# Retention and FP4 feed-forward: old state read in row halves, queries, scores and state moved up in VectorE's order

## What is computed

```python
qkv = x @ w_qkv.T                                  # q, k: 8 heads of 32; v: 8 heads of 64
q, k = xpos(q), xpos(k)                            # rotation and scale by position
ret = einsum('bhtd,bhsd->bhts', q, k) * 32**-0.5 * decay[h]**(t-s)   # for s <= t, else 0
out = einsum('bhts,bhsv->bhtv', ret, v)
y = silu(x @ w_gated.T) * (out - mean) / sqrt(var + eps) @ w_proj.T  # mean, var per head
x1 = layernorm(x + y)
# feed-forward, 704 hidden, every operand rounded to FP4 in blocks of 16 with a scale each
h = silu(q4(x1) @ q4(w_gate).T) * (q4(x1) @ q4(w_up).T)
result = layernorm(x1 + q4(h) @ q4(w_down).T)
```

## Time and profile before

| | us |
|---|---|
| median of 3 runs | 621.46 (619.71 to 621.79) |
| the profiled execution | 620.8, its span 619.0 |
| TensorE busy | 583.0 (94%), 4304 instructions |
| its weight loads | 499.7 (81%) |
| VectorE busy | 518.0 (84%), 1293 |
| ScalarE busy | 338.2 (55%), 834 |
| GpSimd busy | 226.3 (37%), 258 |
| chain that ended last | PE 48%, issue 17%, DVE 16%, ACT 12% |

### The profile page before, as it was taken

How to read it: one execution, slowest core, us unless ns; L and a number is a source line. 1 busy time by engine, 2 the same in 40 slices (tenths; PEclk the granted TensorE clock), 3 DMA queues, 4 the chain that set the end, 5 groups by cost and what they waited for, 6 DMA issues and landing times.

```text
span 619.0 us, 13802 instructions
## 1 busy us (share of the span) xinstructions
PE 583.0 (94%) x4304; PEld 499.7 (81%) x4304; DVE 518.0 (84%) x1293; ACT 338.2 (55%) x834; POOL 226.3 (37%) x258
## 2 busy tenths in 40 slices
PE   7999999999999999999999787878999999999984
PEld 3788888788878888787878666767999999999984
DVE  6668788889889888988898767888888888888896
ACT  3356566675757666676757652413444545445442
POOL 2110123343433434343433205445454455444520
PEclk9999999999999999999999978987999999999998
DMA  7610111011011101100110000000000101010002
GB/s 208 205 44 10 52 52 36 19 51 51 6 44 51 42 8 51 51 25 25 51 34 10 17 11 1 0 2 0 1 19 17 35 2 35 1 36 17 18 19 85
DMA packets 24966, 22.30 MB, mean 36 GB/s; under 512 B 2009, under 2 KB 21858, under 8 KB 24930
## 3 DMA queue, kind: packets, MB, share of 16 engines
q1 hardware_dynamic: 24114, 20.27, 10.9%
q10 hardware_dynamic: 816, 1.57, 0.8%
HBM read 17.63 MB, written 4.20 MB: 35 GB/s over the span
## 4 chain that ended last, share of the span: by engine, by line
PE 48%; issue 17%; DVE 16%; ACT 12%; POOL 3%; DMA 2%; DVEq 1%; ACTq 0%; POOLq 0%
PE wide_banks L1291 24%; PE upd_y L1291 7%; ACT shared L441 5%; PE mixed L1291 5%; PE mixed L1354 3%; PE wide_banks L1464 3%; ACT shared L456 2%; PE mixed L1347 2%; ACT squares L433 2%; DVE stats L648 1%; DVE resid L644 1%; PE wide_banks L1338 1%; POOL shared L1259 1%; POOL shared L1264 1%; ACT x_rounder L403 1%
## 5 line engine op out<-in xcount | busy, mean ns | idle before, releaser
L1264 POOL TENSOR_TENSOR shared<-shared,h_scale 128x704 f32<-128x704 bf16 x31 | 43.0, 1389 | 84.7 <-DVE shared L814 84.7
L527 ACT ACTIVATE shared<-wide_banks 128x512 f32<-128x512 f32 x64 | 29.6, 463 | 80.1 <-PE wide_banks L1291 80.1
L441 ACT ACTIVATE shared<-opened,rstd 128x64 f32<-128x64 f32 x256 | 64.7, 335 | 13.5 <-DVE rstd L727 13.1
L1291 PE MATMUL wide_banks<-wgu_hi,xq_hi 128*128 128x512 f32 (+1 forms) x192 | 61.8, 404 | 9.0 <-DVE xq_lo L1015 9.0
L1291 PE MATMUL wide_banks<-win_hi,x_hi 128*128 128x512 f32 x192 | 67.9, 435 | 0.4 <-DVE shared L637 0.4
L1354 PEld LDWEIGHTS mixed<-shared 128*128 128x128 f32 x512 | 62.0, 192 | 2.8
L1354 PE MATMUL mixed<-shared 128*128 128x64 f32 x512 | 60.6, 271 | 0.0
L1291 PE MATMUL wide_banks<-win_hi,x_lo 128*128 128x512 f32 x192 | 60.4, 396 | 0.0
L1291 PE MATMUL wide_banks<-win_lo,x_hi 128*128 128x512 f32 x192 | 60.3, 395 | 0.0
L1215 POOL TENSOR_TENSOR x_lo<-xf,x_hi 128x256 fp32r<-128x256 f32 x32 | 23.8, 743 | 99.3 <-DVE rsq L712 50.0
L1259 POOL TENSOR_TENSOR shared<-shared,h_inv 128x704 f32<-128x704 f32 x31 | 43.1, 1392 | 44.5 <-DVE h_inv L805 44.5
(11 more groups left out here) (149 smaller groups left out, 1463.6 us busy)
## 6 DMA issues: line engine op xcount, KB each, us to landing
xf<-in_x_feat SPq DMA_DIRECT2D x32, 128.0 KB, 2.2
tab<-in_tables SPq DMA_DIRECT2D x16, 256.0 KB, 2.7
xt<-in_x_tok SPq DMA_DIRECT2D x32, 128.0 KB, 2.1
out<-x SPq DMA_DIRECT2D x32, 128.0 KB, 1.7
x<-in_w_in ACTq DMA_DIRECT2D x3, 512.0 KB, 5.4
w<-in_w_gu SPq DMA_DIRECT2D x1, 1408.0 KB, 8.4
w<-in_w_down SPq DMA_DIRECT2D x1, 704.0 KB, 9.6
wgu_lo<-pow_dram SPq DMA_DIRECT2D x1, 576.0 KB, 4.5
```

The source lines that it names most:

```text
L441: last = act.activation(gated[:, b, cols], opened[:, b, cols], ACT.Copy, scale=rstd[:, b, 1 + k:2 + k])
L527: act.activation(silu[:, cols[0]:cols[1]], proj[:, part, 0:cols[1] - cols[0]], ACT.Silu).then_inc(silu_done[part], 1)
L1264: pool.tensor_tensor(over_blocks(hq[:, b]), over_blocks(h_steps[:, b]), spread(h_fp4["scale"][:, b]), ALU.mult).then_inc(h_fp4["ready"], 1)
L1291: last = pe.matmul(dst, lhs, rhs, start=k == 0, stop=k == len(parts) - 1)
```

## The change

- **State in row halves.** `state_bd` has 128 columns per group and not 256: heads 0 and 1 of a group keep rows 0 to 63, heads 2 and 3 rows 64 to 127, and both pairs use the same 128 columns. `cross` has four matmuls of 64 rows and 128 columns in place of two of 128 rows and 256 columns. The row halves r = 0 and r = 1 write different banks.
- **Banks.** `mixed` is the upper 256 columns of banks 5 and 6; `upd` is in the lower columns of bank 6; `y` is in the upper columns of bank 4, one of the scores' (for the last three tiles, in bank 6). The heads stand in another order in `mixed` (function `place`), so `gate` is read and `w_proj` is loaded (two DMAs, waited for as 32) in that order.
- **Waits.** `upd_done` is signalled by cross's last matmul and not by update's. `mix` waits for `state_summed` of the same tile; `update` waits for `opened_ready`; `scores` waits for `resid_done`, in place of `update`; `project_out` waits for `ret_ready` and no longer for `state_summed`. GpSimd's `split_x` waits for `qd_ready`, in all tiles, in place of a joint step in the even ones.
- **VectorE's order.** decay_q and decay_scores stand right behind joint_var and joint_guess, ahead of x_scale, w_scale and the inverses; sum_state stands ahead of w_unit and w_exponent and of split_gated; joint_fine and joint_fine_square stand behind split_gated.

```diff
@@ -82,6 +82,12 @@
+def place(h):
+    g, j = divmod(h, PER)
+    return PER * (j // 2) + 2 * g + j % 2
 def retention_ffn(nc, x_tok, x_feat, w_in, w_proj, w_gu, w_down, decay, tables, eye, pow_dram, out):
         def sb(name, shape, dt=F32):
@@ -95,13 +101,12 @@
         turn = psum("turn", [P, BANK])
-        wide_banks = psum("wide_banks", [P, 5, BANK])
+        wide_banks = psum("wide_banks", [P, 7, BANK])
         proj, score = wide_banks[:, 0:3], wide_banks[:, 3:5]
         row_scores = wide_banks[:, 1:5, 0:GROUPS * P]
-        mixed = psum("mixed", [P, BANK])
-        upd_y = psum("upd_y", [P, GROUPS * DV + DM])
-        upd = upd_y[:, 0:GROUPS * DV].rearrange("p (g v) -> p g v", v=DV)
-        y = upd_y[:, GROUPS * DV:]
+        mixed = wide_banks[:, 5:7, DM:BANK]
+        y = score[:, 1, DM:BANK]
+        upd = wide_banks[:, 6, 0:GROUPS * DV].rearrange("p (g v) -> p g v", v=DV)
         ident = sb("ident", [P, P])
@@ -132,7 +137,7 @@
         rot, vs, gate, gated, state_bd, ret, dmask = views(
-            shared, (2, 2 * QK), (2, VD), (2, VD), (2, VD), (2, GROUPS, PER * DV), (HEADS, P), (HEADS, P))
+            shared, (2, 2 * QK), (2, VD), (2, VD), (2, VD), (2, GROUPS, 2 * DV), (HEADS, P), (HEADS, P))
         xf = sb("xf", [P, 2, KC, P])
         x_lo = sb("x_lo", [P, 2, KC, P], F32R)
@@ -248,6 +253,7 @@
         turned_h, fresh_up = flat(score)[:, 0:FC * P], flat(proj[:, 1:3])[:, G1:G1 + FF]
+        halves = lambda t: t.rearrange("p (r c) -> p r c", r=2)
         head_cols = lambda t: t.rearrange("p (h v) -> p h v", v=DV)
         over_blocks = lambda t: t.rearrange("p (b e) -> p b e", e=BLOCK)
@@ -288,9 +294,13 @@
+        def y_of(n):
+            return wide_banks[:, 6, 0:DM] if isinstance(n, int) and n >= TILES - LAG else y
         def z_of(b):
-            return (y if b else mixed[:, 0:DM])
+            return wide_banks[:, 5 + b, 0:DM]
@@ -351,7 +361,8 @@
             load_xf(1, 1)
-            sp.dma_start(wproj[:], w_proj.rearrange("(c p) n -> p c n", p=P)).then_inc(ld_proj, 16)
+            for r in range(2):
+                sp.dma_start(wproj[:, 2 * r:2 * r + 2], w_proj.rearrange("(g r p) n -> r p g n", g=GROUPS, p=P)[r]).then_inc(ld_proj, 16)
             sp.dma_start(w4_gu, w_gu.rearrange("(r p) k -> p r k", p=P)).then_inc(ld_w4, 16)
             load_tab(1)
@@ -430,7 +441,7 @@
                 need(act, heads_summed, n)
-                act.activation(squares[:], mixed[:], ACT.Square, scale=DV ** -0.5).then_inc(squared, 1)
+                act.activation(halves(squares[:]), mixed, ACT.Square, scale=DV ** -0.5).then_inc(squared, 1)
                 act.wait_ge(rstd_ready, n + 2 - b)
@@ -453,7 +464,7 @@
                     rows = slice(DQ * j, DQ * (j + 1))
-                    last = act.activation(state_bd[rows, b, :, DV * j:DV * (j + 1)], state[rows, b], ACT.Copy)
+                    last = act.activation(state_bd[rows, b, :, DV * (j % 2):DV * (j % 2 + 1)], state[rows, b], ACT.Copy)
                 last.then_inc(state_placed, 1)
             def body(n, b, piece):
@@ -478,7 +489,7 @@
                 if isinstance(n, int) and n == 0:
-                    act.wait_ge(ld_proj, 16)
+                    act.wait_ge(ld_proj, 32)
                     act.activation(wproj_hi[:], wproj, ACT.Copy).then_inc(wproj_hi_ready, 1)
                     square_heads(n)
@@ -641,7 +652,7 @@
                 need(dve, x1_ready, n - 1)
-                dve.tensor_tensor(resid[:, b], y, xt[:, b], ALU.add).then_inc(resid_done, 1)
+                dve.tensor_tensor(resid[:, b], y_of(n), xt[:, b], ALU.add).then_inc(resid_done, 1)
                 dve.wait_ge(resid_done, n + 1)
@@ -651,7 +662,8 @@
                 need(dve, gated_ready, n - 1)
-                dve.tensor_tensor(opened[:, b], mixed[:], gate[:, b], ALU.mult).then_inc(opened_ready, 1)
+                dve.tensor_tensor(opened[:, b].rearrange("p (r g c) -> p r g c", r=2, g=GROUPS), mixed.rearrange("p r (g c) -> p r g c", g=GROUPS),
+                                  gate[:, b].rearrange("p (g r c) -> p r g c", g=GROUPS, r=2), ALU.mult).then_inc(opened_ready, 1)
                 need(dve, resid_stats_done, n - LAG + 1)
@@ -818,6 +830,10 @@
                     joint_guess(n)
+                if valid(n):
+                    decay_q(n)
+                if valid(n):
+                    decay_scores(n)
                 if x:
                 if w and b == 1:
@@ -826,25 +842,22 @@
                     w_inverse(piece)
-                if valid(n):
-                    decay_q(n)
                 if joint:
                     joint_product(n)
-                    joint_fine(n)
-                    joint_fine_square(n)
-                if valid(n):
-                    decay_scores(n)
+                if carried(n):
+                    sum_state(n, b)
                 if w and b == 1:
...
                     split_gated(n - LAG)
+                if joint:
+                    joint_fine(n)
                 for group in weights(n, 0):
                     turn_weights(group)
-                if carried(n):
-                    sum_state(n, b)
                 if joint:
+                    joint_fine_square(n)
                     joint_fine_product(n)
                     joint_root(n)
@@ -1190,9 +1203,9 @@
-            def behind_fine(n):
-                pool.wait_ge(joint_step, NORM_STEPS // 2 * (n - 2) + 6)
+            def behind_queries(n):
+                pool.wait_ge(qd_ready, n + 1)
@@ -1228,8 +1241,8 @@
                 if valid(n + 2) and not (isinstance(n, int) and n < 0):
-                    if b == 0 and valid(n - 2):
-                        behind_fine(n)
+                    if valid(n - 2):
+                        behind_queries(n)
                     split_x(n + 2, b)
                     behind_x_exponent(n - 1)
@@ -1332,6 +1345,7 @@
                 need(pe, ret_ready, n)
+                need(pe, resid_done, n - LAG)
                 for g in range(GROUPS):
                         rows = slice(DQ * j, DQ * (j + 1))
@@ -1344,15 +1358,22 @@
                 for g in range(GROUPS):
-                    pe.matmul(mixed[:, PER * DV * g:PER * DV * (g + 1)], qdT[:, g], state_bd[:, b, g],
-                              start=g == 0, stop=False, skip_group_check=True)
+                    for r in range(2):
+                        rows = slice(2 * DQ * r, 2 * DQ * (r + 1))
+                        last = pe.matmul(mixed[:, r, 2 * DV * g:2 * DV * (g + 1)], qdT[rows, g], state_bd[rows, b, g],
+                                         start=g == 0, stop=False, skip_group_check=True)
+                if carried(n):
+                    last.then_inc(upd_done, 1)
...
                 pe.wait_ge(ret_ready, n + 1)
+                if carried(n):
+                    pe.wait_ge(state_summed, n + 1)
                 for k in range(HEADS):
-                    last = pe.matmul(mixed[:, DV * k:DV * (k + 1)], ret[:, slot(k)], vs[:, b, DV * k:DV * (k + 1)],
-                                     start=False, stop=k == HEADS - 1, skip_group_check=True)
+                    r, at = place(k) // PER, place(k) % PER
+                    last = pe.matmul(mixed[:, r, DV * at:DV * (at + 1)], ret[:, slot(k)], vs[:, b, DV * k:DV * (k + 1)],
+                                     start=False, stop=k >= HEADS - 2, skip_group_check=True)
                 last.then_inc(out_done, 1)
             def update(n, b):
@@ -1360,13 +1381,12 @@
                 need(pe, state_summed, n)
-                need(pe, resid_done, n - LAG)
+                need(pe, opened_ready, n)
                 for g in range(GROUPS):
                         k = PER * g + j
-                        last = pe.matmul(upd[DQ * j:DQ * (j + 1), g], kd[:, DQ * k:DQ * (k + 1)], vs[:, b, DV * k:DV * (k + 1)],
-                                         start=True, stop=True)
-                last.then_inc(upd_done, 1)
+                        pe.matmul(upd[DQ * j:DQ * (j + 1), g], kd[:, DQ * k:DQ * (k + 1)], vs[:, b, DV * k:DV * (k + 1)],
+                                  start=True, stop=True)
                 pe.wait_ge(gated_ready, n + 1)
@@ -1383,8 +1403,11 @@
                 need(pe, resid_done, n)
-                pe.wait_ge(state_summed, n + LAG + 1 if not isinstance(n, int) else min(n + LAG + 1, TILES - BATCH))
-                accumulate(y, [(t[:, P * c:P * (c + 1)], w[:, c]) for t, w in
+                if isinstance(n, int) and n >= TILES - LAG:
+                    pe.wait_ge(opened_ready, TILES)
+                else:
+                    pe.wait_ge(ret_ready, n + LAG + 1)
+                accumulate(y_of(n), [(t[:, P * c:P * (c + 1)], w[:, c]) for t, w in
                                ((gatedT_hi, wproj_hi), (gatedT_hi, wproj_lo), (gatedT_lo, wproj_hi)) for c in range(VC)]).then_inc(y_done, 1)
             def body(n, b, piece):
@@ -1426,7 +1449,7 @@
             for _ in range(WARM):
```

(2 more changed lines are left out.)

## The result

The changed kernel takes 626.92 us (median of 4 runs, 626.09 to 628.54) against 621.21 (619.71 to 621.79): ratio 1.0099, 95% interval 1.0072 to 1.0126. It is slower by 5.7 us, where 630.4, or +8.9, was forecast. The profiled execution took 626.09, its span is 624.3 (before: 620.8 and 619.0). In experiment 3 one run of nine took 703.17 us at a mean granted clock of 0.748; its ratio leaves that run out, its median does not.

What follows compares the result with a forecast made beforehand. The VectorE/ScalarE ring was taken to bound the loop, and TensorE tiles 0 to 7. Eleven pairs at +1.04 (+11.4), tiles 0 to 7 (-1.7) and tile 30 (-0.8) gave +8.9, 630.4 us; range 621 to 636.

Steps and rivals of the forecast that it cites:

- The ring: Loop, tiles 8 to 29: VectorE and ScalarE work closes the 21.40 us period without gaps; a faster TensorE wins nothing.
- The other signs: Loop: scores period 22.2 to 22.6 us; w_exponent 1.3 to 1.7 later against scores; tiles 3 to 7 at 10.2 to 10.4.
- VectorE's two waits: In the loop VectorE waits for upd_done in even tiles (0.45 us) and for the scores in odd ones (0.36).
- TensorE's stall ahead of turn_gated: Loop, even tiles: TensorE stalls about a microsecond ahead of turn_gated.
- Cross: Cross product, each tile: next group 0.69 us after its start, last end at 0.73; bounds 0.43 and 1.12 us.
- Tiles 0 to 7: Early TensorE-bound tiles: 0.21 us saved per tile, -1.7 us over eight, -2.9 at most.
- Odd tile: Loop, batch row 1: x_max's end (T) to w_exponent's end grows 0.59 us: sum_state 0.38, idle 0.36, less 0.15.
- Even tile: Loop, batch row 0: VectorE waits 0.45 us for upd_done, now signalled by the last cross matmul; segment +0.45.
- Tile 30: Behind the loop: project_v comes 0.6 us sooner; with 0.2 from tile 31's cross, -0.8 us.
- Sum: Whole kernel: eleven pairs at +1.04 (+11.4), -1.7 and -0.8 give net +8.9 us, 630.4 us.
- the second stage: Second stage of the kernel: no change, since z keeps two banks of its own.

Runs made afterwards that it cites:

- experiment 3: Kernel before, with the two cross matmuls of each tile left out and mix starting the sum: 625.39 us, ratio 1.0060.
- experiment 2: Changed kernel with VectorE's old order and split_x's old wait put back; row halves, banks and new waits stay: 618.54 us, ratio 0.9962.
- experiment 4: Changed kernel with ScalarE's place_state moved ahead of round_w: 613.76 us, ratio 0.9885.
- Experiment 5: Changed kernel with sum_state of the loop's tiles put back behind w_unit and w_exponent: 625.38 us, ratio 1.0079.
- experiment 1: Kernel before with VectorE's new order and GpSimd's split_x behind qd_ready alone; cross, banks and their waits stay: 631.79 us, ratio 1.0162.
- experiment 10: Changed kernel with small quantiser steps between decay_q and decay_scores in odd tiles, and joint_fine and joint_fine_square ahead of sum_state in even ones: 624.76 us.
- experiment 6: Changed kernel with joint_fine and joint_fine_square ahead of sum_state in even tiles: 630.24 us, ratio 1.0154.
- experiment 9: Changed kernel with x_scale, w_scale and the two inverses between decay_q and decay_scores in odd tiles: 626.59 us, ratio 1.0098.

## Why the prediction was right, point by point
- **The ring, and that TensorE's gain is lost in the loop: shown**, by experiments 2, 3 and 4. It was worked out from VectorE and ScalarE alone, and in the kernel before that is the ring that decides. For the changed kernel that is only part of it: the prediction names ScalarE and VectorE for its chain, and TensorE has the largest part, over 40%.
- **The other signs.** Come true: VectorE's two waits, TensorE's stall ahead of turn_gated (1.39) and the 10.3 us of tiles 3 to 7. Missed: the period is 22.15, just under 22.2, and w_exponent ends 1.06 us later against the scores (4.00 for 2.94), where 1.3 to 1.7 was given.
- **Cross.** Forecast 0.69 us to the next group and 0.73 to its end; measured 0.65 and 0.71. The pace of the scores was the right row to go by.
- **Tiles 0 to 7.** The second pair of project_v was forecast 2.82 behind the scores of tile 7, and came there:

```profile
86.59 0.73 PE L1352 MATMUL wide_banks<-qkT 32*128 32x128 f32 x16
...
88.20 0.71 PE L1363 MATMUL wide_banks<-shared,qdT 64*128 64x128 f32 x8
...
89.41 0.63 PE L1304 MATMUL wide_banks<-win_lo,x_hi 128*128 128x512 f32 x2
```

Tiles 3 to 7 give 0.27 each on the mean. But tiles 0 to 2 give nothing. I had counted eight tiles from one that is not like the first three. Those have no turn_gated, so project_v already waited for decay_scores (L648), and it still does, 2.15 us behind the scores:

```profile
27.84 0.73 PE L1352 MATMUL wide_banks<-qkT 32*128 32x128 f32 x16
...
28.62 1.22 DVE L648 TENSOR_TENSOR shared<-wide_banks,shared 128x1024 f32<-128x1024 f32 x1 [0.63 <-PE wide_banks L1352]
...
29.99 0.70 PE L1304 MATMUL wide_banks<-win_hi,x_hi 128*128 128x512 f32 x2 [0.42 <-DVE shared L648]
```

The Trainium skill, "TensorEngine Tiling (Array Packing)", section "PSUM Bottleneck", says that tiling makes TensorE faster but not the reading of PSUM, which may then be the bound. In these tiles the trace agrees: cross is 0.4 shorter, and project_v still waits for the 1.22 us of decay_scores, which reads PSUM.
- **Odd tile, +0.59 forecast, +0.10 measured.** The mechanism was right, three sizes were off. decay_scores starts at T + 0.46 and not at T + 0.70, since the even tile was longer than forecast and so the scores earlier against VectorE; the small steps take 0.75 and not 0.92 (two gaps among them, 0.16 from start to start, are now 0.08; why was not followed); sum_state takes 0.29 and not 0.38. Experiment 5 puts its true price in the ring at 0.15. In experiment 1, where TensorE is not relieved, the same stretch grows by 0.94.
- **Even tile, +0.45 forecast, +0.64 measured.** sum_state starts 0.22 behind the end of cross, not 0.06, and that is most of it. The end is a modelled one, and in the odd tile of experiment 10 the same distance is 0.05, so 0.22 is not a fixed price of the signal. But the step was wrong in kind: the prediction added this wait and the odd tile's idle time as two terms. They are the two sides of one balance. A longer even tile takes VectorE to the odd one later, where the scores are then done sooner relative to it. Experiments 6, 9 and 10 show it: each term removed alone gives nothing or 0.1, both together 0.2. The sum, +1.04 per pair, was 0.29 too high. In it the odd tile was 0.49 too high and the even one 0.19 too low; how much of that is the wrong kind of sum and how much the three sizes was not separated.
- **Tile 30.** Forecast: project_v 0.6 sooner after resid_moments. Measured: 2.17 us (340.29 to 342.46), before 2.83 (333.57 to 336.40).

```profile
340.12 0.17 DVE L675 BATCH_NORM_AGGREGATE moments<-stats 128x2 f32<-128x6 f32 x1
...
342.46 0.73 PE L1304 MATMUL wide_banks<-win_hi,x_hi 128*128 128x512 f32 x2
```

- **Sum.** The span grew by 5.3 us and not by 8.9. The even tiles' scores are a poor mark for the loop: they used to start 0.30 behind resid_moments (205.17 to 205.47) and now start 1.13 ahead of it (206.24 to 207.37), so they show 1.4 us of TensorE's lead that the ring never gained. By VectorE's own marks the account closes. At the end of tile 30's resid_moments the kernel is 6.72 us behind (333.57 to 340.29), where 9.7 was forecast: 3.2 of the difference are the period (11 pairs by 0.29), and against it tiles 0 to 7 gave 1.45 and not 1.7. From there to the last pair's joint_root 0.9 comes back (361.59 to 367.42, +5.83), forecast 0.8. Before, and then after:

```profile
333.40 0.17 DVE L663 BATCH_NORM_AGGREGATE moments<-stats 128x2 f32<-128x6 f32 x1
...
361.41 0.18 DVE L727 SCALAR_TENSOR_TENSOR rstd<-poly,fine 128x18 f32<-128x18 f32 x1
```

```profile
367.24 0.18 DVE L739 SCALAR_TENSOR_TENSOR rstd<-poly,fine 128x18 f32<-128x18 f32 x1
```

The last 0.5, from +5.8 to +5.3, falls in the second stage, which the forecast put at no change; luck, so far as the rows go. There TensorE's granted clock falls at other places in the two profiles: it is 0.76 in 418 to 432 us before and 0.88 in the same work after (424.7 to 438.7), and the distance, which had grown to +6.7 by then, goes to +5.3 over that stretch and the next.

## What to carry to other kernels
Before a matmul is made faster, close the ring: if the works of two engines, laid end to end through their waits, sum to the period with no idle time in them, the third only keeps step, however busy it looks. The idle time matters, since any closed path that contains its waits sums to the period. When something is moved ahead of a wait, ask what used to fill that wait, and whether another engine, idle in front of one late signal, has work behind it that could go first: here moving 1.25 us of ready work in front of ScalarE's wait was worth 13 us. In the kernel before, the same move was worth 1 us, since TensorE sets the period there at 21.30. And idle times that lie on two rings of nearly one length aren't a sum: here each filled alone gave at most 0.1, both together 0.2.

## What the runs showed of the hardware
TensorE's granted clock fell in the middle of a kernel in which it was busy over 90% of the time. In experiment 6 it does so in two of eleven pairs; columns as in the earlier trace rows, the clock ahead of the last two:

```profile
120.00:142.00 22.00, 20.59 (x188) 17.23 (x188) 18.60 (x51) 14.08 (x40) 8.39 (x11) 1.00 0.11 36
142.90:146.40 3.50, 3.50 (x26) 2.72 (x15) 2.44 (x12) 1.86 (x7) 0.00 (x0) 0.52 0.00 0
```

For some 3.5 us it is 0.52 of full speed, the 1.2 GHz level but for the edges, and cross takes 1.18 us and not 0.71:

```profile
142.06 0.63 PE L1397 MATMUL turn<-ident,shared 128*128 128x128 f32 x4 [1.38 <-DVE qdT L640]
...
142.98 1.18 PE L1362 MATMUL wide_banks<-shared,qdT 64*128 64x128 f32 x8
```

Ahead of the lower clock TensorE had stood idle 1.38 us for decay_q, as it does in every pair of this kernel and (1.39) of the changed one, whose loop has no such dip in the profile. All four runs of experiment 6 have a mean clock of 0.974 or 0.975, those of the changed kernel 0.976 to 0.983. Experiment 3, which leaves out matmuls, shows a dip too, behind waits of 0.50 and 0.87 us. A dip costs 1.5 us, as much as two pairs of the loss studied here. Why it comes in one pair and not in the next is left open. The rows show that it follows such gaps, not that the gaps bring it about.
